# The delta-rule stage of a decoder on one NeuronCore: two inverses in flight, and two 64-row products on all four tiles

## The reference

```python
mixed_qkv = einsum('bsh,ch->bcs', hidden_states, Wqkv)
mixed_qkv = silu(causal_depthwise_conv(mixed_qkv, conv_w))     # 4 taps
query, key_, value = split(mixed_qkv)      # 16 key heads, 32 value heads, 128 wide
beta = sigmoid(b); g = -exp(A_log) * softplus(a + dt_bias)
def step(state, inp):                      # over the 64 tokens
    q_t, k_t, v_t, g_t, b_t = inp          # q and k l2-normalised
    state = state * exp(g_t)
    kv_mem = einsum('bhkv,bhk->bhv', state, k_t)
    state = state + k_t * ((v_t - kv_mem) * b_t)
    out = einsum('bhkv,bhk->bhv', state, q_t)
core_n = core * rsqrt(mean(core * core) + EPS) * norm_w * silu(z)
return einsum('bsv,hv->bsh', core_n, Wout)
```

## Time and profile before

| | |
|---|---|
| three runs | 4779.5, 4787.9, 4791.57 us; median 4787.9 |
| span of the profiled execution | 4786.8 us; the page gives no other time for it |
| the stage (first project to last add to X) | 2238.7 to 4132.1 us |
| busy over the whole span | TensorE 86%, VectorE 68%, ScalarE 44%, GpSimd 32% |

### The profile page before, as it was taken

The page is one execution under the profiler, slowest core; times in us unless marked ns, Lnnn a source line. Parts: engine busy times, 40 slices in busy tenths (PEclk is TensorE's granted clock), DMA queues, the critical chain, the costliest instruction groups (busy, mean ns, idle before and its releaser), DMA issues. The chain is left out here.

```text
span 4786.8 us, 142961 instructions
## 1 busy us (share of the span) xinstructions
PE 4133.9 (86%) x62052; PEld 2708.2 (57%) x62052; DVE 3251.6 (68%) x6025; ACT 2096.0 (44%) x3703; POOL 1514.4 (32%) x1605
## 2 busy tenths in 40 slices
PE   7627886677767887997999999999999999789999
PEld 6415654323325664444677777777777777455555
DVE  7897745788897886754677777777777777531111
ACT  3446533544444554323555555555555555221111
POOL 1001200298893220000443334433344433112222
PEclk9869997888898998998999999999999999789999
DMA  1000000133341001001000000000010000041111
GB/s 34 19 27 11 2 12 20 67 121 119 120 141 37 2 2 34 20 1 40 15 21 21 21 24 21 21 21 21 21 26 23 21 17 4 8 128 53 49 53 44
DMA packets 72967, 175.11 MB, mean 37 GB/s; under 512 B 14578, under 2 KB 27892, under 8 KB 69748
## 3 DMA queue, kind: packets, MB, share of 16 engines
q1 hardware_dynamic: 72340, 165.96, 11.1%
HBM read 163.04 MB, written 2.88 MB: 35 GB/s over the span
## 5 line engine op out<-in xcount | busy, mean ns | idle before, releaser
L1721 POOL TENSOR_TENSOR ssm_ub<-ssm_dtu,ssm_bcn 128x512 f32<-128x512 f32 x256 | 324.4, 1293 | 299.5 <-DMA ssm_bcn<-ssm_bct 297.1
L2485 POOL TENSOR_TENSOR dn_eb<-dn_ee,dn_cc 128x512 f32<-128x512 f32 x64 | 66.7, 1042 | 1034.2 <-DVE dn_cc L2599 1034.2
L3030 DVE TENSOR_TENSOR moe_hh<-moe_si,moe_pu 128x512 f32<-128x512 f32 x104 | 71.4, 688 | 450.5 <-PE moe_pu L2919 444.3
L2527 DVE SCALAR_TENSOR_TENSOR core_XN<-dn_bA,dn_w,core_XN 128x504 f32<-128x504 f32 (+2 forms) x384 | 280.6, 731 | 24.9 <-ACT core_XN L2361 4.9
L1620 ACT ACTIVATE ssm_da<-core_XN,ssm_al 128x504 f32<-128x504 f32 x240 | 163.2, 683 | 253.5 <-DVE ssm_ph L1788 169.0
L2982 POOL TENSOR_TENSOR moe_hw<-moe_hh,moe_cb 128x512 f32<-128x512 f32 x100 | 126.6, 1266 | 444.2 <-DVE moe_hh L3030 392.7
L2963 ACT ACTIVATE moe_si<-moe_pg 128x512 f32<-128x512 f32 x104 | 62.1, 597 | 467.7 <-PE moe_pg L2919 467.7
L2191 PE MATMUL dn_bA<-core_XT,dn_w 128*128 128x512 f32 x512 | 258.8, 629 | 9.0 <-ACTq L2453 4.4
L1608 PE MATMUL ssm_py<-ssm_hc,core_ident 128*128 128x512 f32 x352 | 200.6, 675 | 61.7 <-DVE ssm_hc L1792 31.2
L2325 PE MATMUL dn_po<-dn_wo,dn_cT 128*128 128x256 f32 x1024 | 242.1, 390 | 2.6 <-issue 1.4
L1788 DVE TENSOR_TENSOR_SCAN ssm_ph<-ssm_da,ssm_ub 128x512 f32<-128x512 f32 x168 | 204.9, 1220 | 29.3 <-POOL ssm_ub L1721 17.1
(11 more groups left out here) (498 smaller groups left out, 10429.9 us busy)
## 6 DMA issues: line engine op xcount, KB each, us to landing
ssm_bcn<-ssm_bct SPq DMA_DIRECT2D x128, 512.0 KB, 3.6
dn_cb<-dn_cum SPq DMA_DIRECT2D x32, 512.0 KB, 5.0
dn_w<-in_dn_w SPq DMA_DIRECT2D x32, 388.0 KB, 3.3
moe_cb<-moe_rows SPq DMA_DIRECT2D x64, 192.0 KB, 2.8
moe_w<-in_moe_w SPq DMA_DIRECT2D x26, 384.0 KB, 7.5
moe_cb<-moe_rows SPq DMA_DIRECT2D x64, 128.0 KB, 3.0
dn_wo<-in_dn_w SPq DMA_DIRECT2D x16, 256.0 KB, 5.2
moe_cb<-moe_rows SPq DMA_DIRECT2D x64, 64.0 KB, 2.6
```

Of the source, the lines that this page charges most:

```text
L1721: pool.tensor_tensor(ub[u % NUB][:, :], dtu[q % 2][:, c, :], bcn[i % NB][:, 0, :], ALU.mult).then_inc(ub_ready, 1)
L2527: last = dve.scalar_tensor_tensor(dst[:, :, n:S], src[:, :, 0:S - n], w[i // NCH % 2][:, at:at + 1], dst[:, :, n:S], ALU.mult, ALU.add)
```

## The change

Steps in flight become four stages instead of three: `new` (i), `mid` (i - 1), `late` (i - 2) and `old` (i - 3). An inverse does levels 1 and 2 and the z round of level 3 in one step and the rest in the next. Its rounds stand in pairs: the z round of one inverse, then the x round of the other, with nothing between. `zz` gets two buffers, PT, vv, sk and rb a third.

TensorE's list becomes M, z1 x3, P1, V, z4 x1, P2, P3, z2 x4, G0, g, z5 x2, G1, T, v0, ssq, z3 x5, v1, y, sst, and P0 of the next step. M and V write po, in bank h, on all four tiles: for h = 1, b's rows go to the other half of the columns in M and come back in V. So that the halves meet, the values of h = 1 are stored with the two sequences of a tile exchanged (`silu_turned`), and sk is stored for both orders (`roots`).

XF is now filled by ScalarE: `diagonal` after level 4, `corner` after level 5. VectorE's conv of gi 3 stands behind the cn multiplies and the norm block, and `values` waits for it (`raw_free`). `y_added` is waited for before M instead of before V. The semaphore `mb_ready` counts once for level 1 and once for the rest. The loop has 64 steps and three more. The diff, cut to its core (declarations, and lines that only move, left out):

```diff
+                        for j in range(TPC):
+                            for h in range(2):
+                                for b in range(BPT):
+                                    at = 1 - b if h else b
+                                    mm = pe.matmul(po[rowsof(at), h, j * S:(j + 1) * S], XF[rowsof(b), 2 * j + h, :],
+                                                   PT[o % 3][rowsof(b), 2 * j + h, :], start=True, stop=True,
+                                                   tile_position=(b * S, at * S))
+                        mm.then_inc(mp_ready, 1)
+                    if late:
+                        take(pe, zz_ready)
                     if mid:
-                        level_z(m, 1)
-                    if new:
+                        level_z(i - 1, 1)
+                    if late:
+                        level_x(i - 2, 3, even)
+                    if new:
+                        if i:
+                            take(pe, tq_done)
                         project(i, 1, bB)
...
+                                    mm = pe.matmul(po[rowsof(b), h, j * P:(j + 1) * P], Mt[rowsof(at), h * TPC + j, :],
+                                                   vv[o % 3][rowsof(at), 2 * j + h, :], start=True, stop=True,
+                                                   tile_position=(at * S, b * S))
                         mm.then_inc(o_ready, 1)
...
+                    if late:
+                        level_z(i - 2, 4)
+                    if mid:
+                        level_x(i - 1, 1, odd)
...
+                    if new:
+                        take(pe, raw_free)
+                        take(pe, silu_ready)
+                        values(0, bA)
+                        take(pe, sq_ready)
+                        take(pe, zs_done)
...
+                    if i + 1 < NSTEP:
+                        take(pe, vv_done)
+                        first(i + 1)
```

```diff
+                def silu_turned(gi):
+                    take(act, conv_ready)
+                    src = acc[:, gi, :].rearrange("p (j b t) -> p j b t", b=BPT, t=S)
+                    dst = cv[:, gi, :].rearrange("p (j b t) -> p j b t", b=BPT, t=S)
+                    for b in range(BPT):
+                        last = act.activation(dst[:, :, 1 - b, :], src[:, :, b, :], ACT.Silu)
+                    last.then_inc(silu_ready, 1)
...
+                def diagonal(m):
+                    take(act, diag_ready)
+                    x = halves(XB[m % 2][:, 1, :])
+                    act.activation(XF[:, :, 0:HB], x, ACT.Copy)
+                    act.activation(XF[:, :, HB:S], x, ACT.Copy, scale=second_half)
+
+                def corner():
+                    take(act, p5_ready)
+                    act.drain()
+                    for b in range(BPT):
+                        low = slice(b * S + HB, (b + 1) * S)
+                        last = act.activation(XF[low, :, 0:HB], halves(pm[low, 1, 0:NS * HB]), ACT.Copy)
+                    last.then_inc(xf_ready, 1)
...
+                def roots(i):
+                    take(act, ssk_ready)
+                    act.activation(lk[:, :], ssk[i % 2][:, :], ACT.Ln)
+                    act.drain()
+                    act.activation(sk[i % 3][:, 0, :], lk[:, :], ACT.Exp, scale=0.5)
+                    for b in range(BPT):
+                        act.activation(sk[i % 3][rowsof(1 - b), 1, :], lk[rowsof(b), :], ACT.Exp, scale=0.5)
```

More of the change, by code:

```diff
@@ L2056, in l3_attn @@
         cT = s.sb("cT", [P, NS, P])
-        zz = s.sb("zz", [P, NS * HB])
+        zz = [s.sb(f"zz{k}", [P, NS * HB]) for k in range(2)]
         Mt = s.sb("Mt", [P, NS, S])
@@ L2102, in schedule @@
         def schedule(step):
-            for i in range(NSTEP + 2):
+            for i in range(NSTEP + 3):
                 step(i)
@@ L2168, in _ @@
                 mm.then_inc(ab_ready, 1)
[L2170 to L2177, removed]
                 def running():
@@ new lines, in first @@
+                def first(i):
+                    if i % NCH == 0:
+                        take(pe, w_loaded[i // NCH % 2], 32)
+                    project(i, 0, bA)
+                def step(i):
+                    new, mid, late, old = i < NSTEP, 0 < i <= NSTEP, 1 < i <= NSTEP + 1, i >= 3
+                    o = i - 3
+                    even, odd = zz[i % 2], zz[(i + 1) % 2]
+                    if i == 0:
+                        first(0)
+                    if old:
+                        take(pe, xf_ready)
+                        take(pe, y_added)
+                        for j in range(TPC):
[12 more added lines that the diff above has]
+                        level_x(i - 2, 3, even)
+                    if new:
+                        if i:
+                            take(pe, tq_done)
@@ L2473, in step @@
                 def step(i):
-                    new, old = i < NSTEP, i >= 2
-                    o = i - 2
-                    if new:
-                        take(pool, ee_ready)
-                        if i + 2 < NSTEP:
-                            decays(i + 2)
-                    if i % NCH == 1 and new:
+                    if i >= NSTEP:
+                        return
+                    take(pool, ee_ready)
+                    if i + 2 < NSTEP:
+                        decays(i + 2)
@@ new lines, in step @@
+                    pool.drain()
+                    pool.tensor_tensor(BD[:, :, :], BD[:, :, :], BL[:, :, :], ALU.add)
+                    pool.drain()
+                    pool.tensor_tensor(b0[:, :, :], BD[:, :, :], bcm(small[:, 1, :], NS), ALU.mult)
+                    pool.drain()
+                    if i >= 2:
+                        take(pool, xf_ready)
+                    pool.tensor_tensor(halves(XB[i % 2][:, 0, :]), b0[:, :, :], bcm(small[:, 0, :], NS), ALU.add).then_inc(xt_ready, 1)
@@ L2501, in _ @@
+                    for l in range(1, NL - 1):
+                        last = pool.tensor_tensor(halves(mb[i % 2][:, l - 1, :]), BD[:, :, :], bcm(small[:, 1 + l, :], NS), ALU.mult)
+                        if l == 1:
+                            last.then_inc(mb1_ready, 1)
+                    last.then_inc(mb_ready, 1)
                 decays(0)
@@ L2600, in step @@
                                           ALU.mult).then_inc(c_ready, 1)
-                        if q == NCH - 1:
-                            dve.sem_inc(w_free, 1)
+                        conv(i, 3, bA)
+                    if mid:
+                        update(i - 1, 2)
+                    if new:
                         take(dve, eb_ready)
@@ L2626, in step @@
                             dve.sem_inc(wo_free, 1)
+                    if new:
+                        take(dve, sst_ready)
+                        dve.tensor_scalar(rb[i % 3][:, :], bB[:, P:2 * P:32], 1e-6, 128e-6, ALU.add, ALU.mult).then_inc(tq_done, 1)
+                        if q == NCH - 1:
+                            dve.sem_inc(w_free, 1)
                 schedule(step)
```

256 lines of the change are left out of this document (112 added, 144 removed).

## The result

The changed kernel takes 4812.6 us (median of four runs, 4807.7 to 4818.4) where the kernel before takes 4786.9: a ratio of 1.0054, with an interval of 1.0040 to 1.0068. It is 0.5% slower. The forecast was 4681, with a range of 4635 to 4735. The profiled execution took 4818.4 us, its span 4816.6.

A forecast was written before the change was run, and what follows sets the result against it. TensorE, never idle, bounded the kernel; afterwards a chain through VectorE's fourth conv would set a 26.8 us step. From 4787.9 us, -114 (intervals), -7 (ramp) and +14 (tail) gave -107: 4681 us, range 4635 to 4735.

The forecast's parts named there:

- Sum: 28.64 - 0.47 - 0.87 - 0.55 - 0.80 = 25.95: TensorE's list per step, less savings on M, V, joined rounds and full-array stretches: 25.95 us if it never waits.
- the walk behind it: VectorE's and TensorE's lists followed from M: 18.76 us to the fourth conv's last read, plus 8.05, gives the step.
- wait at v0: Once per step TensorE waits 0.91 us before v0 until VectorE's fourth conv has read bank A.
- M and V: The two 64x64 products on four tiles instead of two: M 0.61 us (-0.47), V 1.02 us (-0.87).
- the joined pair: Two rounds of different inverses run back to back on TensorE: 1.25 us, saving 0.55 us a step over five pairs.
- the step of 26.8: One loop step, P1 to P1, falls from 28.64 to 26.8 us; over 62 intervals -114 us.
- The ramp: Steps 1 and 2, not step 1 alone, run without old products: an estimated -7 us.
- the tail: After the last projects, a third step is added by the step in flight: 91 us estimated, +14 us.
- TensorE alone: Rival: VectorE packs closer and the v0 wait goes; 25.95 to 26.3 us a step, 4628 to 4650 us; chance 0.08.
- No more than two tiles: Rival: M and V stay 1.08 and 1.89 us; 27.3 to 27.6 us a step, 4715 to 4735 us; chance 0.08.
- A longer chain: Rival: X add, z stalls or ScalarE's XF copies add 0.5 to 1.5 us a step; 4710 to 4770 us; chance 0.16.
- The clock: Rival: waiting at v0 lowers TensorE's granted clock; gain lost at 6.4% half-clock work, 4880 us at 12%; chance 0.07.

The follow-up runs named there:

- e5: The changed kernel plus useless filling instructions (17 products before v0 each step, 60 once in step 0), making a step 6 x 256 instructions: 4684.2 us, ratio 0.9797.
- e6: The kernel of e5 with 33 one-time filling products in place of 60, putting a 256-instruction boundary in the middle of x3: 4848.9 us (one run).
- e1: The kernel before with only the two products M and V on four tiles, one inverse at a time: 4735.2 us, ratio 0.9896.
- e7: As e6 with 9 one-time filling products, putting a boundary in the middle of x1 behind V and z4: 4889.4 us (one run).
- e3: The changed kernel with rounds of levels 1 to 4 in products twice as wide, half the instructions: 4669.7 us (one run).

## Why the prediction was wrong

- **The step that failed** is "Sum: 28.64 - 0.47 - 0.87 - 0.55 - 0.80 = 25.95. This is TensorE's demand if it never waits", and with it the walk behind it. Every wait I priced was on another engine. That TensorE's own instructions must arrive has no term in it, though the change packs 320 of them into 2 us, and no rival named it. The missing term is 62 x 2.2 us = 136, where time and forecast are 132 apart.
- **Its size, by parts** (stretch of 60.1 steps): gaps at the places of 256, without the one that is a wait at v0, are 114.3 / 60.1 = 1.90 us a step. P1 and P2 take 139.8 / 60 and 133.9 / 60 us where they took 1.98 each: 0.60 for the clock after a stall. The wait at v0 is 0.56, where the five undisturbed intervals have 0.75, as a late TensorE waits less: -0.19. Sum 2.31, measured 28.96 - 26.76 = 2.20; the sum is a little too high, since a gap from start to start holds the ordinary distance too.
- **Shown right:** M and V; the joined pair; that VectorE's list up to the fourth conv sets the step, with a wait at v0 (0.75 us in undisturbed intervals, 0.91 forecast; in e5, behind some 0.5 us of filling, 0.44, and the filling lengthens the interval by only 0.1); the step of 26.8, which undisturbed intervals have and which e5 has with 26.9. The ramp and the tail came out near the forecast as wholes; their parts were estimates and were not read, so the match may be luck. In e5 the terms are -108.6 for the 62 intervals (2272.29 to 3939.14, below), -7.7 for the ramp and +12.1 for the tail, against -114, -7 and +14.

```profile
2272.29 3.30 PE L2185 MATMUL dn_bB<-core_XT,dn_w 128*128 128x512 f32 x4
...
3939.14 1.98 PE L2185 MATMUL dn_bB<-core_XT,dn_w 128*128 128x512 f32 x4
```

- **The rivals.** TensorE alone: no, it still waits at v0. No more than two tiles: no, 0.63 and 1.04 us, though two row tiles write into each bank. A longer chain: no such wait appeared; what looks like one is inside a round. The clock: in part. It does fall, 25 times from 2320 to 3920 us, but each time behind an issue stall, never behind the wait for v0, and in P1 and P2 it is 0.60 of the 2.2 us. These rows, by form, are P1 of e5 and P1 of e6, with its boundary in the round ahead:

```profile
L2185 PE MATMUL dn_bB<-core_XT,dn_w 128*128 128x512 f32 x244 | 121.0, 618 | 0.0
```

```profile
L2185 PE MATMUL dn_bB<-core_XT,dn_w 128*128 128x512 f32 x232 | 169.0, 870 | 0.0
```

The warning was in the trace of before: seven issue stalls of 0.2 to 0.6 us in the stretch, four of them in the rounds, all at places of 256. I saw TensorE never idle and read nothing from it on what feeds it.

## What to carry to other kernels

The last brought 2.0% against before (e5), though it holds only as long as nothing changes the count ahead of it. The part that needs no such care (e1) brought 1.0%.

## What the runs showed of the hardware

- TensorE's instructions came in packets of 16 KB, 256 instructions of 64 bytes (489 packets, 8.01 MB; 128 packets fewer for 32,768 instructions fewer). The Trainium skill (Runtime: NRT & Kernel Launch, Instruction fetch mechanics) says the same of the block, and that crossing a boundary is "mostly hidden". In the kernel before it was, with 8.4 us in 349 places; in the changed one it cost 115.8 us in 343.
- When a block was used up in 1.4 us (e6), TensorE went on 3.4 us after the block had begun. In nine kernels no boundary was passed sooner than 1.19 us after the end of the packet before it; a packet took 0.9 to 2.3 us and began mostly some 1 us behind its boundary (median 1.04 in the changed kernel), but up to 7.0 us behind. What decides when a packet begins stays open: for eleven blocks of before that took 2.4 us it began between 0.7 us ahead of the boundary and 0.8 us behind it, so no long wait followed.
- After about half of the stalls of some 2 us (25 times for 48 long ones from 2320 to 3920 us of the changed kernel) the clock was granted at the lower level for a few matmuls: four of 512 columns took 3.56 us in place of 1.98. From 3024 to 3030 us of e7, behind its stall in x1, it is 0.72 in the mean, where TensorE is busy all the time:

```profile
3024.00:3030.00 6.00, 6.00 (x76) 2.66 (x77) 4.33 (x7) 3.04 (x6) 0.00 (x0) 0.72 0.01 3
```

Behind e3's waits at v0 the same fall shows in seven of 59 cases, after waits of 1.4 to 1.8 us; its P1 and P2 matmuls, further on, take 618 ns, as before. Behind the shorter waits at v0 of e5 (0.4 us) and of the changed kernel (0.6) it never shows. So the wait that I feared was harmless at its size, and the one that I had not seen was not.
